# Gated feed-forward of a decoder block: activations in two float32r parts in place of three bf16 ones, three sets of gate and up banks, two banks for the down products

## The chip, the cores and the metric

The kernel runs on one core of one Trainium2 chip. The metric is the device time of one execution in microseconds; the median of three runs is 887.89 us (886.81 to 888.18). Engines: TensorE (PE in the profile, its weight loads PEld), VectorE (DVE), ScalarE (ACT), GpSimd (POOL) and SyncE (SP), which here only issues DMAs.

## The reference

Eight batches of 256 tokens with 256 features go through two decoder layers: a gated recurrence, a cross attention, a ternary feed-forward, a self attention with relative positions, a masked cross attention, and last a gated feed-forward. Only the last is touched. Per batch, with x the output of the masked attention after its layer norm:

```
gate = x @ (Wg_int / 127).T          # 256 -> 768
up   = x @ (Wu_int / 127).T          # 256 -> 768
y    = x + (silu(gate) * up) @ (Wd_int / 127).T     # 768 -> 256
out  = layernorm(y)
```

The weights are integers from -127 to 127, which bf16 holds exactly. Activations are float32. The kernel before writes each activation as a sum of three bf16 numbers (high, middle, low), multiplies all three by the weights and adds up in PSUM, so that the product is as good as a float32 one.

## The kernel before

The work is ordered by hand: each engine has its own program, and semaphores tie them. The feed-forward (in `attention_mask`, L1343 and on) works on pairs of batches: 512 tokens are one matmul's moving side. There are four pairs and six blocks of 128 hidden features (HT = 6), so 24 groups n = 6 p + m.

- **gate_up(n)**, TensorE, L1473: 6 matmuls for gate and 6 for up (two halves of the 256 features, three parts), 128x128 weights against 512 tokens, into banks 2 (n mod 2) and 2 (n mod 2) + 1. It waits until the products of group n-2 have read these banks.
- **tanh(n)**, ScalarE, L1708: tanh of the gate bank.
- **hidden(n)**, VectorE, L1820: two products, (tanh + 1) * gate (L1824) and that times up (L1830), into one of two buffers `hid_two`. The second waits for lo_made of group n-2, that is until GpSimd has read the buffer.
- **high(n)** on ScalarE (L1715, bf16 copy), **rest(n)** on VectorE (L1834, hidden minus high), **middle(n)** on ScalarE (L1721, bf16 copy of the rest), **low(n)** on GpSimd (L1962, rest minus middle, to bf16).
- **down(t)**, TensorE, L1500: for batch t, 2 token tiles x 6 blocks x 3 parts = 36 matmuls, the activation block stationary, 256 columns of the weights moving. It waits for all six low(n) of the pair. Banks 4 to 7 are used in turn.
- **out_begin(t)**, **out_end(t)**, VectorE, L1840 and L1867: residual, statistics, normalisation; **out_inverse(t)** on GpSimd between them (L1969).
- **split_x(b, i)**, GpSimd, L1945: the four steps that write the three parts of x of batch b. **cast_weights** (L1937) turns the integers into bf16 during batch 1 of the attention.

The order on ScalarE in the loop over n:

```python
                for n in range(1, NG):
                    tanh(n)
                    ...
                    middle(n - 1)
                    high(n)
```

VectorE does rest(n-1) and then hidden(n); out_begin follows hidden(n) for n mod 6 = 3 and 4, out_end for n mod 6 = 5 and 0. The first groups are mixed with the last attention batch: gate_up(0) stands in `fourth_round(7)`, gate_up(1) before weigh(31) (L1600), and up to gate_up(5) TensorE has turn_back, transposes and the output projection of batch 7 between the groups. VectorE has normalise(7, 0) and (7, 1) after hidden(2) and hidden(3), and norm_begin of batch 7 after hidden(5). GpSimd has normalise(7) after low(4). down(2p-2) stands after gate_up(6p+2) and down(2p-1) after gate_up(6p+3). At the end down for batches 6 and 7 runs over blocks 0 to 3 first, then 4 and 5 as their low parts come.

Of the kernel before, what the change touches and what calls it, by code (L numbers as in the profile page):

```python
# [17 lines left out]
BF16 = mybir.dt.bfloat16  # L18
I32 = mybir.dt.int32
# [7 lines left out]
P = 128  # L27
B, S, D = 8, 256, 256
H, DH = 16, 16
HID = 768  # L30
# [65 lines left out]
def decoder_kernel(nc, xT, ctxT, fside, mask0, mask1, wmats, cols_d, rows_d, gb, gate_up, down,  # L96
                   ident_d, rel_k_d, rel_v_d, mix_d, consts_d, out):
    ctx = ExitStack()
    with ctx:
# [9 lines left out]
        zero_cell = sb("zero_cell", [1, 1])  # L109
        x_feat = sb("x_feat", [P, FT, B * S])  # L110
        x_tok = sb("x_tok", [P, B, TT, D])
        c_feat = sb("c_feat", [P, FT, B * S])
        w_all_mats = sb("w_all_mats", [P, len(WMATS), FT, D])
        W = {n: w_all_mats[:, i, :, :] for i, n in enumerate(WMATS)}
# [120 lines left out]
        def glu_weights():  # L235

            return (dist[:, 0, 0:6, :].rearrange("p h s -> p (h s)").rearrange("p (k n) -> p k n", k=FT),
                    dist[:, 0, 6:12, :].rearrange("p h s -> p (h s)").rearrange("p (k n) -> p k n", k=FT),
                    dist[:, 1, 0:6, :])

        dist = sb("dist", [P, TT, H, S])
        ones_w = sb("ones_w", [P, P])
        bnd = sb("bnd", [P, TT, H * NBAND])
        dist_pairs = dist[:, :, :, :].rearrange("p t h s -> p t (h s)")\
            .rearrange("p t (e s v) -> p t e s v", e=H // 2, v=2)
        rw = sb("rw", [P, TT, H // FT // 2, RW, 2])
# [1096 lines left out]
        def attention_mask(sa_y_mm, sa_y_steps, sa_biased, sa_kept, sa_xt_mm, sa_xt_sb, sa_r_out):  # L1343
# [14 lines left out]
            x_steps, w_cast, g_mm, u_mm, th_sb, prod, h_made, hi_sb, r_made, mid_sb, lo_made = (  # L1358
                sem(f"glu_{n}") for n in ("x_steps", "w_cast", "gate_mm", "up_mm", "tanh", "product", "hidden",
                                          "high", "rest", "middle", "low"))  # L1360
# [3 lines left out]
            w_cells = rw[:, :, :, :, :].rearrange("p t e w v -> p (t e w v)")[:, 0:3 * FT * HID // 2].bitcast(BF16)  # L1364
# [3 lines left out]

            def cells(area, pattern):

                return area.rearrange(pattern).bitcast(BF16)

            x_parts = [cells(a, "p h s -> p (h s)").rearrange("p (k n) -> p k n", k=FT)
                       for a in (dist[:, 1, H // 2:H, :], dist[:, 0, 0:H // 2, :], dist[:, 0, H // 2:H, :])]
            PAIR = 2 * S
            h_high = cells(w_all_mats[:, 2:8, :, :], "p i k n -> p (i k n)").rearrange("p (a m t) -> p a m t", a=2, m=HT)
            h_mid = c_feat[:, :, :].rearrange("p k n -> p (k n)")[:, 0:HT * PAIR].bitcast(BF16)\
                .rearrange("p (a m t) -> p a m t", a=2, m=HT)
            h_low = [cells(dist[:, 1, 0:HT, :], "p h s -> p (h s)").rearrange("p (m t) -> p m t", m=HT),
                     bnd[:, :, :].rearrange("p t w -> p (t w)")[:, 0:HT * S].bitcast(BF16)  # L1380
                     .rearrange("p (m t) -> p m t", m=HT)]
# [8 lines left out]
            def part_of(part, n, lo, hi):  # L1390

                p, m = divmod(n, HT)
                if part == 2:
                    return h_low[p % 2][:, m, lo:hi]
                return (h_high, h_mid)[part][:, p % 2, m, lo:hi]

            def down_bank(t, tt):

                if t < B - 2:
                    return bank[4 + t % 4][:, tt * D:(tt + 1) * D]  # L1400
                return bank[((6, 7), (4, 5))[t % 2][tt]][:, 0:D]
# [32 lines left out]
            def mask_pe(pe):  # L1434
# [38 lines left out]
                def gate_up(n):  # L1473
# [17 lines left out]
                def down_steps(t, tt, ks):  # L1491

                    p, lo = t // 2, t % 2 * S + tt * P
                    for k in ks:
                        for i in range(3):
                            last = pe.matmul(down_bank(t, tt), part_of(i, HT * p + k, lo, lo + P), w_down[:, k, :],  # L1496
                                             start=(k == 0 and i == 0), stop=(k == HT - 1 and i == 2))
# [147 lines left out]
            def mask_act(act):  # L1645
# [62 lines left out]
                def tanh(n):  # L1708
# [3 lines left out]
                    act.activation(th_two[n % 2], bank[2 * (n % 2)][:, :], ACT.Tanh, scale=0.5 * UNIT)\  # L1712
# [20 lines left out]
                for n in range(1, NG):  # L1733
# [7 lines left out]
                    middle(n - 1)  # L1741
                    high(n)
                middle(NG - 1)

            def mask_dve(dve):
# [74 lines left out]
                def hidden(n):  # L1820
# [4 lines left out]
                                             in1=bank[2 * (n % 2)][:, :], op0=ALU.add, op1=ALU.mult)\  # L1825
# [5 lines left out]
                                             in1=bank[2 * (n % 2) + 1][:, :], op0=ALU.mult, op1=ALU.mult)\  # L1831
                        .then_inc(h_made, 1)

                def rest(n):  # L1834

                    dve.wait_ge(hi_sb, n + 1)
                    dve.tensor_tensor(hid_two[n % 2], hid_two[n % 2], part_of(0, n, 0, PAIR), ALU.subtract)\
                        .then_inc(r_made, 1)

                def out_begin(t):  # L1840
# [5 lines left out]
                    if t < B - 2:  # L1846
                        step(dve.scalar_tensor_tensor(
                            out=y_two[i][:, :, :], in0=bank[4 + t % 4][:, :].rearrange("p (t f) -> p t f", t=TT),
# [30 lines left out]
                for n in range(1, NG):  # L1879
                    rest(n - 1)  # L1880
# [16 lines left out]
                rest(NG - 1)  # L1897
# [6 lines left out]
            def mask_pool(pool):  # L1904
# [40 lines left out]
                def split_x(b, i):  # L1945

                    whole = batch(x_feat, b)
                    high, mid, low = (batch(part, b) for part in x_parts)
                    if i == 0:
                        pool.wait_ge(xt_sb, b + 1)  # L1950
                        pool.wait_ge(w_cast, 3)
                        pool.tensor_copy(high, whole).then_inc(x_steps, 1)
                        return
                    pool.wait_ge(x_steps, 4 * b + i)
                    if i == 1:
                        pool.tensor_tensor(whole, whole, high, ALU.subtract).then_inc(x_steps, 1)
                    if i == 2:
                        pool.tensor_copy(mid, whole).then_inc(x_steps, 1)
                    if i == 3:
                        pool.tensor_tensor(low, whole, mid, ALU.subtract).then_inc(x_steps, 1)  # L1960
# [15 lines left out]
                for b in range(B):  # L1976
# [7 lines left out]
                    if b >= 3:  # L1984
                        for i in range(4):
# [4 lines left out]
                for n in range(NG):  # L1990
# [1190 lines left out]
```

## Time and profile before

| | |
|---|---|
| median of 3 runs | 887.89 us (886.81 to 888.18) |
| span of the profiled execution | 885.5 us, clock 0.999 |
| TensorE busy | 847.8 us (96%), 7018 instructions |
| VectorE busy | 680.2 us (77%) |
| ScalarE busy | 618.7 us (70%) |
| GpSimd busy | 417.6 us (47%) |

The profiled execution's span counts from its first to its last instruction; the run's time lies 2.4 us above it. Busy shares are averages over six layers with different limits; the feed-forward is the stretch from about 774 us to the end.

### The profile page before, as it was taken

To read this page: it belongs to the slowest core of one execution; us is meant where nothing else is said; L and a number is where in the kernel's file an instruction comes from. 1 tells how busy PE (TensorE), PEld (TensorE's weight loads), DVE (VectorE), ACT (ScalarE), POOL (GpSimd) and SP (SyncE) were. 2 spreads that over 40 slices of the span, in tenths; PEclk is the share of its full clock that TensorE was granted. 3 is DMA by queue.
4 is the path that set the end of the run, shared out by engine and by line. 5 is a ranking of instruction groups with operands and counts; after the bars stand their busy time and mean duration, and the time that the engine had idled before them with its cause. 6 is when DMAs were issued, how large, how long until landed. Compare 5 with 4: busy or idle time off the path is not lost.

```text
span 885.5 us, 21124 instructions
## 1 busy us (share of the span) xinstructions
PE 847.8 (96%) x7018; PEld 613.6 (69%) x7029; DVE 680.2 (77%) x2504; ACT 618.7 (70%) x1605; POOL 417.6 (47%) x447
## 2 busy tenths in 40 slices
PE   9998999999989989999999999999999999999996
PEld 7876777777768667777676766767666766746554
DVE  4988798888997767787686766838888888866876
ACT  4547877777872578787787777748888888854441
POOL 1256546775451345435455342245445555346532
PEclk9999999999999999999999999999999999999999
DMA  9444100000005388797796877760010000000001
GB/s 323 138 119 120 46 24 26 26 25 14 14 13 215 96 279 267 228 283 229 213 283 204 269 231 231 202 210 4 28 29 28 28 29 26 2 1 1 25 24 48
DMA packets 96993, 101.89 MB, mean 115 GB/s; under 512 B 26910, under 2 KB 92190, under 8 KB 96631
## 3 DMA queue, kind: packets, MB, share of 16 engines
q1 hardware_dynamic: 96324, 100.20, 36.4%
q8 instruction: 58, 0.95, 0.4%
q14 instruction: 49, 0.39, 0.2%
q10 hardware_dynamic: 562, 0.35, 0.1%
HBM read 48.70 MB, written 51.82 MB: 114 GB/s over the span
## 4 chain that ended last, share of the span: by engine, by line
PE 46%; ACT 7%; DMA 5%; DVE 4%; issue 2%; SPq 2%; POOL 1%; DVEq 0%; ACTq 0%
PE bank L1445 6%; PE bank L223 5%; PE bank L1486 5%; PE bank L231 4%; PE bank L1429 4%; PE bank L2144 3%; PE bank L1496 3%; PE bank L1460 2%; PE bank L2130 2%; PE bank L2161 2%; ACT bias_area L2482 2%; PE bank L2194 2%; PE bank L2238 2%; PE bank L2232 1%; DMA dist<-skew_scratch 1%
## 5 line engine op out<-in xcount | busy, mean ns | idle before, releaser
L223 PE MATMUL bank<-x_feat,w_all_mats 128*128 128x256 f32 x384 | 93.2, 387 | 2.1 <-ACT q_full L341 0.6
L2879 POOL TENSOR_TENSOR bnd<-bnd,consts 128x60 f32<-128x60 f32 x64 | 18.1, 305 | 142.5 <-DMA bnd<-band_scratch 142.5
L223 PEld LDWEIGHTS bank<-x_feat,w_all_mats 128*128 128x128 f32 x384 | 70.3, 190 | 15.1 <-ACT rw L2524 3.8
L2482 ACT ACTIVATE bias_area<-bias_area,mq_two 128x256 f32<-128x256 f32 x128 | 66.4, 531 | 0.0
L1486 PE MATMUL bank<-dist,rw 128*128 128x512 bf16 x277 | 63.1, 379 | 0.6
L866 ACT ACTIVATE q_heads<-bank 128x512 f32<-128x512 f32 x64 | 37.7, 589 | 34.6 <-PE bank L682 34.6
L2658 DVE COPY q_heads<-bank 128x512 f32<-128x512 f32 x64 | 41.3, 683 | 22.4 <-PE bank L2144 22.4
L1764 DVE COPY q_heads<-bank 128x512 f32<-128x512 f32 x64 | 42.1, 685 | 19.3 <-PE bank L1445 19.2
L1651 ACT ACTIVATE Sx<-Sx,mq 128x256 f32<-128x256 f32 x128 | 54.3, 499 | 3.4 <-DVE mq L1756 3.4
L858 ACT ACTIVATE Sx<-Sx,mq 128x256 f32<-128x256 f32 x128 | 54.4, 498 | 3.0 <-DVE mq L944 3.0
L952 DVE COPY q_heads<-bank 128x512 f32<-128x512 f32 x64 | 41.9, 684 | 18.3 <-PE bank L682 18.3
L858 ACT ACTIVATE Pr<-Pr,mq 128x256 f32<-128x256 f32 x128 | 54.3, 501 | 0.9 <-DVE mq L944 0.9
L1651 ACT ACTIVATE Pr<-Pr,mq 128x256 f32<-128x256 f32 x128 | 54.4, 503 | 0.0
L1756 DVE CUSTOM_DVE_ANT_0 Sx<-bank,bias_area 128x256 f32<-128x256 f32 x128 | 46.6, 421 | 7.4 <-PE bank L1429 4.1
L2500 ACT ACTIVATE w_all_mats<-bank 108x512 f32<-108x512 f32 x32 | 19.0, 595 | 46.7 <-PE bank L2176 46.7
L1659 ACT ACTIVATE q_heads<-bank 128x512 f32<-128x512 f32 x64 | 37.7, 590 | 19.1 <-PE bank L1445 18.5
L944 DVE CUSTOM_DVE_ANT_0 Sx<-bank,bias_area 128x256 f32<-128x256 f32 x128 | 46.5, 420 | 4.7 <-PE bank L668 4.2
L1486 PEld LDWEIGHTS bank<-dist,rw 128*128 128x128 bf16 x288 | 28.2, 98 | 31.3
L231 PE MATMUL bank<-w_all_mats,aT 128*128 128x256 f32 x192 | 46.9, 387 | 1.4 <-ACT q_full L881 1.3
L2650 DVE CUSTOM_DVE_ANT_0 bias_area<-bank,dist 128x256 f32<-128x256 f32 x128 | 46.7, 421 | 1.2 <-DMA dist<-skew_scratch 1.0
L944 DVE CUSTOM_DVE_ANT_0 Pr<-bank,bias_area 128x256 f32<-128x256 f32 x128 | 46.9, 419 | 0.0
L1756 DVE CUSTOM_DVE_ANT_0 Pr<-bank,bias_area 128x256 f32<-128x256 f32 x128 | 46.5, 420 | 0.0
(288 smaller groups left out, 2451.9 us busy)
## 6 DMA issues: line engine op xcount, KB each, us to landing
dist<-skew_scratch SPq DMA_DIRECT2D x64, 296.0 KB, 4.4
skew_scratch<-rw SPq DMA_DIRECT2D x30, 588.0 KB, 4.4
bnd<-band_scratch SPq DMA_DIRECT2D x64, 108.0 KB, 2.8
band_scratch<-bias_area SPq DMA_DIRECT2D x32, 162.0 KB, 2.9
band_scratch<-bias_area SPq DMA_DIRECT2D x32, 148.0 KB, 2.6
skew_scratch<-dist SPq DMA_DIRECT2D x4, 1024.0 KB, 8.4
context_values<-dist SPq DMA_DIRECT2D x8, 512.0 KB, 2.6
v_two<-context_values SPq DMA_DIRECT2D x8, 512.0 KB, 3.5
```

The costliest lines, as they stand in the source:

```text
L223: last = pe.matmul(dst[:, m * S:(m + 1) * S], w[:, k, m * P:(m + 1) * P], rhs[:, k, :], start=(k == 0), stop=(k == FT - 1))
L231: last = pe.matmul(dst[:, t * D:(t + 1) * D], src[:, k, t * P:(t + 1) * P], w[:, k, :], start=(k == 0), stop=(k == FT - 1))
L858: last = act.activation(rows_of(g, t), rows_of(g, t), ACT.Exp, bias=mq[:, g, t:t + 1], scale=-1.0)
L944: dve.tensor_tensor_reduce(out=rows_of(g, t), in0=s_bank[g][:, t * S:(t + 1) * S], in1=bias_two[:, b % 2, t, :], scale=-1.0, scalar=3e38, ...
L952: dve.tensor_copy(PTq[:, 4 * (n % 2) + g, :, :], t_bank[g % 2][:, :].rearrange("p (k q) -> p k q", k=TT))\
L1445: last = pe.transpose(t_bank[g % 2][:, k * S + t * P:k * S + (t + 1) * P], rows_of(g, t)[:, k * P:(k + 1) * P], ident[:, :])
L1486: last = pe.matmul(dst[:, :], w_[:, k, m * P:(m + 1) * P], x_parts[i][:, k, p * PAIR:(p + 1) * PAIR], start=(k == 0 and i == 0), stop=(k = ...
L1651: last = act.activation(rows_of(g, t), rows_of(g, t), ACT.Exp, bias=mq[:, g, t:t + 1], scale=-1.0)
L1756: dve.tensor_tensor_reduce(out=rows_of(g, t), in0=s_bank[g][:, t * S:(t + 1) * S], in1=x1_bias_two[:, b % 2, t, :], scale=-1.0, scalar=3e3 ...
L1764: dve.tensor_copy(PTq[:, 4 * (n % 2) + g, :, :], t_bank[g % 2][:, :].rearrange("p (k q) -> p k q", k=TT))\
L2482: last = act.activation(rows_of(n, g)[:, t, :], rows_of(n, g)[:, t, :], ACT.Exp, bias=mq_two[:, n % 2, g, t:t + 1], scale=-1.0, accum_out= ...
L2650: dve.tensor_tensor_reduce(out=rows_of(n, g)[:, t, :], in0=s_bank[g][:, t * S:(t + 1) * S], in1=dist_pairs[:, t, 2 * j + g // 2, :, g % 2] ...
```

## The change

The parts become two numbers of type float32r, a four-byte type that an engine rounds to when it writes it: high = round(value), low = value - high. All 12 matmuls of gate_up become 8, the 36 of down(t) become 24. rest(n) and middle(n) go; low(n) is hidden minus high and follows high(n). split_x has two steps instead of four. The weights are cast in place (int32 to float32r in `dist`), and the parts lie in other areas, so some buffers are laid out in another order. gate and up have three sets of banks (0 to 5), down two banks (6 and 7; for the last batch 0 and 1). x parts have room for two pairs, so the split of pair p waits for the up products of pair p-2.

```diff
-                        pe.wait_ge(x_steps, 4 * 2 * (p + 1))
-                    for w_, dst, done, free in ((w_gate, bank[2 * (n % 2)], g_mm, prod),
-                                                (w_up, bank[2 * (n % 2) + 1], u_mm, h_made)):
-                        ge(pe, free, n - 1)
+                        pe.wait_ge(x_steps, 2 * 2 * (p + 1))
+                    for w_, dst, done, free in ((w_gate, gate_bank(n), g_mm, prod), (w_up, up_bank(n), u_mm, h_made)):
+                        ge(pe, free, n - 2)
                         for k in range(FT):
-                            for i in range(3):
+                            for i in range(2):
                                 last = pe.matmul(dst[:, :], w_[:, k, m * P:(m + 1) * P],
-                                                 x_parts[i][:, k, p * PAIR:(p + 1) * PAIR],
-                                                 start=(k == 0 and i == 0), stop=(k == FT - 1 and i == 2))
+                                                 x_two[p % 2][:, i, k, :],
+                                                 start=(k == 0 and i == 0), stop=(k == FT - 1 and i == 1))
...
                     for k in ks:
-                        for i in range(3):
+                        for i in range(2):
                             last = pe.matmul(down_bank(t, tt), part_of(i, HT * p + k, lo, lo + P), w_down[:, k, :],
...
                     pe.wait_ge(lo_made, HT * (t // 2 + 1))
-                    ge(pe, n_steps2, 4 * (t - 4) + 1)
-                    if t == 3:
+                    ge(pe, n_steps2, 4 * (t - 2) + 1)
+                    if t == 1:
                         pe.wait_ge(xt_sb, B)
...
+            def gate_bank(n):
+
+                return bank[2 * (n % 3)]
+
+            def up_bank(n):
+
+                return bank[2 * (n % 3) + 1]
...
-                def middle(n):
-
-                    act.wait_ge(r_made, n + 1)
-                    act.activation(part_of(1, n, 0, PAIR), hid_two[n % 2], ACT.Copy).then_inc(mid_sb, 1)
...
-                    middle(n - 1)
                     high(n)
-                middle(NG - 1)
...
-                def rest(n):
-
-                    dve.wait_ge(hi_sb, n + 1)
-                    dve.tensor_tensor(hid_two[n % 2], hid_two[n % 2], part_of(0, n, 0, PAIR), ALU.subtract)\
-                        .then_inc(r_made, 1)
...
                 for n in range(1, NG):
-                    rest(n - 1)
                     hidden(n)
...
+                        ge(pool, u_mm, HT * (p - 1))
+                        pool.tensor_copy(high, batch(x_feat, b)).then_inc(x_steps, 1)
+                    else:
+                        pool.wait_ge(x_steps, 2 * b + 1)
+                        pool.tensor_tensor(low, batch(x_feat, b), high, ALU.subtract).then_inc(x_steps, 1)
...
                 def low(n):
 
-                    pool.wait_ge(mid_sb, n + 1)
+                    pool.wait_ge(hi_sb, n + 1)
                     ge(pool, d_mm, 2 * (n // HT - 1))
-                    pool.tensor_tensor(part_of(2, n, 0, PAIR), hid_two[n % 2], part_of(1, n, 0, PAIR), ALU.subtract)\
+                    pool.tensor_tensor(part_of(1, n, 0, PAIR), hid_two[n % 2], part_of(0, n, 0, PAIR), ALU.subtract)\
                         .then_inc(lo_made, 1)
...
-                    if b >= 3:
-                        for i in range(4):
+                    if 3 <= b < B - 1:
+                        for i in range(2):
                             split_x(b - 3, i)
...
-                    if n in (0, 1, 2, 4):
-                        split_x(B - 3, (0, 1, 2, 4).index(n))
-                    if n in (5, 6, 7, 8):
-                        split_x(B - 2, (5, 6, 7, 8).index(n))
-                    if n in (11, 12, 13, 14):
-                        split_x(B - 1, (11, 12, 13, 14).index(n))
+                    for b, after in ((B - 4, 6), (B - 3, 8), (B - 2, 12), (B - 1, 14)):
+                        if n in (after, after + 1):
+                            split_x(b, n - after)
```

## Rows read from the trace of the kernel before

**Rows 1.** The core's span and its mean granted TensorE clock.

```profile
core 0: 885.5 us, clock 0.999
```

**Rows 2.** Busy time by stretch: PE, PEld, DVE, ACT, POOL; clock, DMA share, GB/s.

```profile
843.40:866.80 23.40, 23.24 (x143) 14.07 (x144) 17.31 (x34) 10.48 (x19) 8.30 (x8) 1.00 0.07 23
866.80:885.50 18.70, 11.55 (x90) 8.51 (x87) 12.47 (x34) 3.97 (x7) 6.30 (x7) 0.94 0.17 57
```

**Rows 3.** Timeline of TensorE: start us, length us, operation, count.

```profile
769.96 1.04 PE L1445 MATMUL bank<-ident,Pr 128*128 128x128 f32 x8
...
796.96 1.89 PE L231 MATMUL bank<-w_all_mats,aT 128*128 128x256 f32 x8
798.69 7.93 PE L1486 MATMUL bank<-dist,rw 128*128 128x512 bf16 x35
806.46 0.60 PE L215 MATMUL bank<-ident,x_tok 128*128 128x128 f32 x4
```

**Rows 4.** The chain that ended last, the last down products.

```profile
870.50 6.56 PE bank L1496 x60
```

**Rows 5.** Timeline of VectorE; in brackets idle time before, and what ended it.

```profile
781.00 0.69 DVE L1824 SCALAR_TENSOR_TENSOR q_par<-k_two,bank 128x512 f32<-128x512 f32 x1 [3.51 <-ACT k_two L1712]
...
798.99 0.69 DVE L182 TENSOR_TENSOR y_sb<-bank,x_tok 128x512 f32<-128x512 f32 x1
...
801.28 0.69 DVE L1837 TENSOR_TENSOR q_par<-q_par,w_all_mats 128x512 f32<-128x512 f32 x1
...
807.97 0.69 DVE L1830 SCALAR_TENSOR_TENSOR q_par<-q_par,bank 128x512 f32<-128x512 f32 x1 [2.70 <-POOL dist L1966]
...
821.80 0.68 DVE L1847 SCALAR_TENSOR_TENSOR at<-bank,x_tok 128x512 f32<-128x512 f32 x1
...
823.74 0.68 DVE L1837 TENSOR_TENSOR q_par<-q_par,w_all_mats 128x512 f32<-128x512 f32 x1
...
825.66 1.14 DVE L1873 TENSOR_SCALAR xn<-y_sb,mv,rstd 128x256 f32<-128x256 f32 x2
...
856.40 0.68 DVE L1824 SCALAR_TENSOR_TENSOR q_par<-k_two,bank 128x512 f32<-128x512 f32 x1
857.11 0.69 DVE L1830 SCALAR_TENSOR_TENSOR q_par<-q_par,bank 128x512 f32<-128x512 f32 x1
...
871.85 0.69 DVE L1830 SCALAR_TENSOR_TENSOR q_par<-q_par,bank 128x512 f32<-128x512 f32 x1
...
877.08 0.76 DVE L1852 SCALAR_TENSOR_TENSOR y_sb<-bank,x_tok 128x256 f32<-128x256 f32 x2 [2.24 <-PE bank L1496]
```

**Rows 6.** Timeline of ScalarE.

```profile
780.38 0.59 ACT L1712 ACTIVATE k_two<-bank 128x512 f32<-128x512 f32 x1
783.51 0.38 ACT L1668 ACTIVATE w_all_mats<-bank 128x256 f32<-128x256 f32 x1 [2.54 <-PE bank L1460]
783.79 0.62 ACT L1719 ACTIVATE w_all_mats<-q_par 128x512 bf16<-128x512 f32 x1
...
855.13 0.63 ACT L1719 ACTIVATE w_all_mats<-q_par 128x512 bf16<-128x512 f32 x1 [0.69 <-DVE q_par L1830]
855.67 0.58 ACT L1712 ACTIVATE k_two<-bank 128x512 f32<-128x512 f32 x1
...
857.84 0.63 ACT L1719 ACTIVATE w_all_mats<-q_par 128x512 bf16<-128x512 f32 x1 [0.69 <-DVE q_par L1830]
```

**Rows 7.** Groups by line and form: busy us, mean ns of a weight load.

```profile
L231 PEld LDWEIGHTS bank<-w_all_mats,aT 128*128 128x128 f32 x192 | 34.7, 190 | 12.0 <-issue 8.1
...
L1486 PEld LDWEIGHTS bank<-dist,rw 128*128 128x128 bf16 x288 | 28.2, 98 | 31.3
L1445 PEld LDWEIGHTS bank<-ident,Pr 128*128 128x128 f32 x256 | 27.8, 141 | 8.5 <-ACT Pr L1651 6.3 <-issue 2.0
```

**Rows 8.** Timeline of GpSimd.

```profile
801.45 1.09 POOL L1929 TENSOR_TENSOR rstd<-ve,neghalf 128x2 f32<-128x2 f32 x1 [2.03 <-DVE ve L197]
...
805.57 1.15 POOL L1960 TENSOR_TENSOR dist<-x_feat,dist 128x512 bf16<-128x512 f32 x1
...
874.94 1.16 POOL L1966 TENSOR_TENSOR bnd<-q_par,c_feat 128x512 bf16<-128x512 f32 x1 [1.12 <-ACT c_feat L1724]
```

More of the change, by code:

```diff
@@ L18 @@
 BF16 = mybir.dt.bfloat16
+F32R = mybir.dt.float32r
 I32 = mybir.dt.int32
@@ L1356, in attention_mask @@
                 s_(n) for n in ("norm_steps", "normed", "y_steps", "rstd", "kept"))
-            x_steps, w_cast, g_mm, u_mm, th_sb, prod, h_made, hi_sb, r_made, mid_sb, lo_made = (
+            x_steps, w_cast, g_mm, u_mm, th_sb, prod, h_made, hi_sb, lo_made = (
                 sem(f"glu_{n}") for n in ("x_steps", "w_cast", "gate_mm", "up_mm", "tanh", "product", "hidden",
-                                          "high", "rest", "middle", "low"))
+                                          "high", "low"))
             d_mm, n_steps2, rstd2, xn_ready = (sem(f"glu_{n}") for n in ("down_mm", "n_steps", "rstd", "xn"))
@@ L1367, in attention_mask @@
             w_down = w_down.rearrange("p (k n) -> p k n", k=HT)
[L1369 to L1381, printed above, removed]
+            x_two = [exact_cells("glu_x_even", [P, 2, FT, PAIR], dist_at + 4 * 3 * FT * HID),
+                     exact_cells("glu_x_odd", [P, 2, FT, PAIR], rw_at)]
+            h_high = [exact_cells("glu_high_even", [P, HT, PAIR], w_all_at + 4 * 2 * FT * D),
+                      exact_cells("glu_high_odd", [P, HT, PAIR], w_all_at + 4 * 8 * FT * D)]
+            low_even = exact_cells("glu_low_even", [P, HT, PAIR], c_feat_at)
+            low_odd = [exact_cells("glu_low_odd_first", [P, HT // 2, PAIR], dist_at + 4 * (3 * FT * HID + 2 * FT * PAIR)),
+                       exact_cells("glu_low_odd_last", [P, HT // 2, PAIR], bnd_at)]
             th_two = [k_two[:, i, :, :].rearrange("p k n -> p (k n)") for i in range(2)]
@@ L1392, in part_of @@
                 p, m = divmod(n, HT)
-                if part == 2:
-                    return h_low[p % 2][:, m, lo:hi]
-                return (h_high, h_mid)[part][:, p % 2, m, lo:hi]
+                if part == 0:
+                    return h_high[p % 2][:, m, lo:hi]
+                if p % 2 == 0:
+                    return low_even[:, m, lo:hi]
+                return low_odd[2 * m // HT][:, m % (HT // 2), lo:hi]
             def down_bank(t, tt):
                 if t < B - 2:
-                    return bank[4 + t % 4][:, tt * D:(tt + 1) * D]
-                return bank[((6, 7), (4, 5))[t % 2][tt]][:, 0:D]
+                    return bank[6 + t % 2][:, tt * D:(tt + 1) * D]
+                return bank[((6, 7), (0, 1))[t % 2][tt]][:, 0:D]
+            def gate_bank(n):
+                return bank[2 * (n % 3)]
+            def up_bank(n):
+                return bank[2 * (n % 3) + 1]
             NQ = H // 4
@@ L1494, in down_steps @@
                     for k in ks:
-                        for i in range(3):
+                        for i in range(2):
                             last = pe.matmul(down_bank(t, tt), part_of(i, HT * p + k, lo, lo + P), w_down[:, k, :],
-                                             start=(k == 0 and i == 0), stop=(k == HT - 1 and i == 2))
+                                             start=(k == 0 and i == 0), stop=(k == HT - 1 and i == 1))
                     return last
@@ L1711, in tanh @@
                     ge(act, prod, n - 1)
-                    act.activation(th_two[n % 2], bank[2 * (n % 2)][:, :], ACT.Tanh, scale=0.5 * UNIT)\
+                    act.activation(th_two[n % 2], gate_bank(n)[:, :], ACT.Tanh, scale=0.5 * UNIT)\
                         .then_inc(th_sb, 1)
@@ L1824, in hidden @@
                     dve.scalar_tensor_tensor(out=gt_two[n % 2], in0=th_two[n % 2], scalar=1.0,
-                                             in1=bank[2 * (n % 2)][:, :], op0=ALU.add, op1=ALU.mult)\
+                                             in1=gate_bank(n)[:, :], op0=ALU.add, op1=ALU.mult)\
                         .then_inc(prod, 1)
@@ L1847, in out_begin @@
                         step(dve.scalar_tensor_tensor(
-                            out=y_two[i][:, :, :], in0=bank[4 + t % 4][:, :].rearrange("p (t f) -> p t f", t=TT),
+                            out=y_two[i][:, :, :], in0=bank[6 + t % 2][:, :].rearrange("p (t f) -> p t f", t=TT),
                             scalar=UNIT, in1=x_tok[:, t, :, :], op0=ALU.mult, op1=ALU.add))
@@ L1945, in split_x @@
                 def split_x(b, i):
-                    whole = batch(x_feat, b)
-                    high, mid, low = (batch(part, b) for part in x_parts)
+                    p, lo = b // 2, b % 2 * S
+                    high, low = (x_two[p % 2][:, part, :, lo:lo + S] for part in range(2))
                     if i == 0:
```

37 lines of the change are left out of this document (18 added, 19 removed).

## The prediction, made before the change was run

> **What bounds the kernel now.** I first looked at the clock and the span: 885.5 us, TensorE at full clock throughout [rows 1]. The change touches only the gated feed-forward, so I then read the stretches of it. One stretch is a pair of batches in the steady part, 843.4 to 866.8: the reader is to see that TensorE is busy 23.24 of 23.40 us while VectorE, ScalarE and GpSimd have 17.3, 10.5 and 8.3 [rows 2]. The stretch behind it, 866.8 to 885.5, is the tail. TensorE's own timeline gives the pace of each form. A bf16 matmul of 512 columns starts 0.216 us after the one before: 36 of them from 798.69 to 806.46, where the next form's row would stand (35 records are shown in 7.93 us, one is missing) [rows 3]. One of 256 columns starts after 6.56/60 = 0.109 us [rows 4]. A pair of batches is 6 x 12 x 0.216 + 2 x 36 x 0.109 = 15.55 + 7.85 = 23.4 us, all of the stretch. So today this part is bound by TensorE's columns and by nothing else.
>
> **But how far off is the next bound?** The answer is not in the busy shares but in an order that the code fixes. ScalarE does tanh(n) and then high(n); high(n) waits for both VectorE products of hidden(n), which wait for tanh(n). tanh(n+1) stands behind high(n) in ScalarE's queue. So each group n is one serial round, however many banks there are. I read its four steps, start to start, where nothing else delayed them: high to the next tanh 855.13 to 855.67 = 0.54; tanh to the first product 780.38 to 781.00 = 0.62; first to second product 856.40 to 857.11 = 0.71; second product to high 857.11 to 857.84 = 0.73 [rows 5, 6]. That is 2.60 us a group. Before, 12 matmuls took 2.59, so the round was hidden.
>
> **The change, part by part.**
> (a) gate_up: 8 matmuls of 512 columns in place of 12. If a float32r matmul moves one column a cycle as bf16 does, a group takes 1.73 us and 24 groups save 24 x 4 x 0.216 = 20.7 us of TensorE time.
> (b) down: 24 of 256 columns per batch in place of 36, 2.62 in place of 3.93 us; 8 x 12 x 0.109 = 10.5 us saved. Together 31.2 us.
> The price of a float32r matmul is the big unknown, since no row has one. The nearest rows are float32: one product of 4 matmuls of 256 columns shows 8 records in 1.89 us, (1.89 - 0.387 for the last one's own length)/7 = 0.215 us each, and two records per matmul [rows 3]. A record thus moves a column in two cycles and a float32 matmul costs four. Ends for float32r: 0.216 us per 512 columns (one cycle) and 0.43 (one record at the float32 pace); above that, at four cycles, the split of the activations would buy nothing. By its bytes the new form is nearest to these rows, by its work to the bf16 ones: float32 takes four cycles for two full operands, that is two halves of each against two of the other; a part that holds about half of an activation's bits, against an integer below 128, is one of the four. I take one cycle. The Trainium skill ("FP8 and Floating Point Precision", TensorE Precision Notes) says the same: true float32 is four passes, reduced precision reads the four bytes and truncates to FP22. By that rule the sum stays at the lower end; four passes agree with the trace's 2 x 0.215 us, the reduced form no row here shows.
> Against the change speaks the weight load of the down products, where a new stationary block comes with every 256 columns. Loads last 0.098 us for bf16, 0.141 in float32 transposes and 0.190 in float32 matmuls [rows 7]; the length is not the pace: 8 float32 transposes, each with its load, take 1.04 us, (1.04 - 0.28)/7 = 0.109 us each [rows 3]. So a four-byte load repeats at least every 0.109 us, and I take 0.109 for a down matmul; the upper end is 0.215. The Trainium skill ("TensorE: Matmul & The Clock Gate", Weight-path perf modes and LDWEIGHTS) says that the fast weight load is off for float32 and that a load is columns/1.2 ns, 107 ns for 128; by that the down matmul would still come at about 0.107, so the rule would not change the sum.
> (c) The third part goes: VectorE's rest(n) (24 instructions of 0.68 us [rows 5]), ScalarE's middle(n) (24 x 0.54) and two of four split_x steps on GpSimd. None of the three engines bounds the stretch [rows 2]; it leaves the round at 2.60 (with rest in it, 855.13 to 857.84 is 2.71 [rows 6]). GpSimd's low(n), 1.16 us, now follows high(n).
> (d) Three sets of banks let TensorE be two groups ahead of the products instead of one. That hides down() behind the round; it doesn't shorten the round. Two banks for down: down(t) needs out_begin(t-2), which is long done in the walk below. down(1) now waits for turn_x(7), since it writes the bank that this reads.
> (e) split_x(4) moves from the last attention batch to groups 6 and 7; split_x(6), (7) to 12 to 15. The weights' cast stays, in place. No DMA moves.
>
> **The walk.** TensorE needs 6 x 1.73 + 2 x 2.62 = 15.6 us a pair. The round needs 6 x 2.60, plus what out_begin adds: VectorE has 2.60 - 1.31 = 1.29 us free in a round, out_begin takes 821.80 to 823.74 = 1.94 [rows 5], so each of two adds 0.66 us. out_end, 1.06 to 1.14 [rows 5], fits. A pair is 15.6 + 1.3 = 16.9 us: the bound has gone from TensorE to the serial round.
> Start: high(0) is at 783.79, right behind the copy that waits for weigh(31) [rows 6]; gate_up(0) and (1) lie before that on TensorE and save 2 x 0.86, so high(0) comes at 782.07. Five rounds: high(5) 795.07, its second product 794.35. Turning back and the two normalise fit in the rounds' gaps. normalise(7, 1) follows group 3's second product (789.15) and I give it until 790.5; transposes 0.66 (three steps of 0.109 and the last one's length), gate_up(5) 1.7, projection 1.9 [rows 3] end by 794.8. Then norm_begin, 2.29 us from 798.99 before, delays the first product of group 6 to 797.25 (a cost of 1.0), and its variance comes 4.0 us earlier than before. GpSimd's normalise(7) holds the queue from 801.45 to 805.57, 4.12 us [rows 8]; now from 797.4 to 801.5. low(5) is queued behind it and ends at 802.7, and the second product of group 7 waits for it, as one waits 2.70 us in the trace before [rows 5]: 802.75, 2.2 late. Group 9: 807.95. down(0) runs 802.8 to 805.4 (it waits for low(5)), gate_up(9) to 807.15, down(1) from 807.8 (turn_x(7)) to 810.4, so gate_up(10) comes 1.6 us late: group 10 at 812.8, group 11, with out_begin(1) in front, at 816.0. Two pairs at 16.9: group 23's second product at 849.9, against 871.85 before [rows 5].
> Tail: high(23) starts 0.73 later and lasts some 0.63 [rows 6], low(23) 1.16 [rows 8]; with the handovers 2.58, 852.45. Before it started 3.1 us after the second product, now 1.4 [rows 5, 8]. TensorE has by then done the 32 down matmuls of parts 0 to 3 (out_begin(5) lets them start near 847.7; 3.5 us). Four more and the last one's result: about 853.3 for the first VectorE read, which is at 877.08 before [rows 5]. From there on nothing changes, 8.4 us. Span 861.7, 23.8 us less. The median of the runs before is 887.9, 2.4 above the span, so 864 us.
>
> **Rivals.**
> 1. The forecast: round bound, 864. Its own bounds: 0.37 us more at each out_begin if its inner waits fall badly, 2 us; as much for contention. 860 to 870. Chance 0.68.
> 2. TensorE stays the bound with nothing lost in waits: 887.9 - 31.2 = 857. For it speaks only the sum of (a) and (b); against it the code's order on ScalarE. It would need a round under 2.6 us. 0.05.
> 3. The down matmuls are bound by their weight loads. They decide from 15.6 + 1.3 = 6 x 1.73 + 48d, d = 0.136 us. At 0.141 to 0.190 (the loads' lengths) a pair is 17.2 to 19.5 us; with the first pair and the tail's 32 about 3 to 11 us more, 867 to 875; at 0.215 it is 8 x 24 x 0.106 = 20.4 less some 5 of slack, 879. 0.13.
> 4. The other side: float32r moves a column in two cycles, as every float32 record does. gate_up is then 24 x (8 x 0.43 - 12 x 0.216) = 20.4 us longer and down 8 x (24 x 0.215 - 36 x 0.109) = 9.9 longer, 918 us; it turns slower from 1.5 cycles a column, where 8 matmuls cost as much as 12. For it: all four-byte rows here; against: the parts argued in (a). 0.14.
>
> **How the numbers follow.** 864 is the likeliest case. Cases 1, 2 and 3 up to 879 hold 0.86; from 858 to 878 about 0.8 is held. Runs before lie from 886.81 to 888.18, so 0.2% is about what can be told from no change. Faster 0.85 (cases 1 to 3), slower 0.14, same 0.01.
>
> **What would show it.** A 512-column float32r matmul at 0.216 us start to start, one record each, and a 256-column one near 0.11. A pair of batches in 16.9 us with TensorE busy about 15.6. tanh waiting for nothing from TensorE but right behind high; rounds of 2.6 us, 3.3 with out_begin. A wait of the second product of group 7 for GpSimd's low(5). The prediction is wrong if records come in pairs or at 0.43 us, or if the round is not 2.6.

## The result and the profile after

The changed kernel takes 865.93 us (median of 4 runs, 863.66 to 869.36) against 887.35 in the same comparison; the ratio is 0.9763, with a 95% interval of 0.9736 to 0.979. It is 21.4 us faster. The prediction was 864.

First the core's span and clock, then busy time by stretch (PE, PEld, DVE, ACT, POOL, clock, DMA share, GB/s), both of the changed kernel. They answer to [rows 1, 2]:

```profile
core 0: 863.6 us, clock 0.995
```

```profile
817.20:834.40 17.20, 17.20 (x100) 15.02 (x99) 13.18 (x29) 6.82 (x12) 12.80 (x13) 1.00 0.09 30
...
851.50:863.60 12.10, 4.16 (x33) 3.75 (x32) 8.09 (x23) 0.63 (x1) 3.00 (x4) 0.90 0.25 87
```

One pair of batches now takes about as long as this stretch, 17.2 us, in place of 23.4, and TensorE is shown as busy all the time in it as before. Busy time alone would say that TensorE still sets the pace. The weight loads have grown to 15.0 of 17.2 us. But the stretch holds 100 matmul records where a pair has 96 matmuls: TensorE gets through a pair's work in less than 17.2 us and runs ahead of the other engines. It had fallen behind them at group 10 and is making that good.

TensorE's timeline of the changed kernel (start, length, count), which answers to [rows 3, 4]:

```profile
823.31 2.00 PE L1501 MATMUL bank<-glu_x_even,glu_weight_cells 128*128 128x512 f32 x8
825.15 0.28 PE L1511 MATMUL bank<-glu_weight_cells,glu_high_odd 128*128 128x256 f32 x1
...
827.88 0.28 PE L1511 MATMUL bank<-glu_weight_cells,glu_low_odd_last 128*128 128x256 f32 x1
828.00 2.23 PE L1501 MATMUL bank<-glu_x_even,glu_weight_cells 128*128 128x512 f32 x9
```

Eight matmuls of 512 columns from 823.31 to 825.15 are 0.230 us each, one record per matmul; the 24 of down(3) from 825.15 to 828.00 are 0.119 each (before: 0.216 and 0.109). A pair is 6 x 8 x 0.230 + 48 x 0.119 = 11.04 + 5.71 = 16.75 us of TensorE.

The weight loads, from the changed kernel's instructions by source line (min/median/max ns), answer to [rows 7]:

```profile
L1501 PEld LDWEIGHTS bank<-glu_x_even,glu_weight_cells x96: 187/188/192, 775.8 to 831.2; 128*128 128x128 f32 x96
```

```profile
L1511 PEld LDWEIGHTS bank<-glu_weight_cells,glu_high_even x48: 186/192/193, 803.1 to 844.5; 128*128 128x128 f32 x48
```

A float32r load lasts as long as one of a float32 matmul (0.190), twice a bf16 one (0.098).

ScalarE's timeline of the changed kernel, answering to [rows 6]:

```profile
812.50 0.60 ACT L1727 ACTIVATE k_two<-bank 128x512 f32<-128x512 f32 x1 [2.60 <-PE bank L1501]
...
837.67 0.63 ACT L1734 ACTIVATE glu_high_odd<-q_par 128x512 fp32r<-128x512 f32 x1 [1.47 <-DVE q_par L1838]
838.21 0.58 ACT L1727 ACTIVATE k_two<-bank 128x512 f32<-128x512 f32 x1
840.27 0.63 ACT L1734 ACTIVATE glu_high_odd<-q_par 128x512 fp32r<-128x512 f32 x1 [1.48 <-DVE q_par L1838]
840.80 0.58 ACT L1727 ACTIVATE k_two<-bank 128x512 f32<-128x512 f32 x1
842.86 0.63 ACT L1734 ACTIVATE glu_high_odd<-q_par 128x512 fp32r<-128x512 f32 x1 [1.48 <-DVE q_par L1838]
```

Here is the serial round: high at 837.67, 840.27, 842.86, so 2.60 us apart; tanh starts 0.54 behind high with no wait of its own, and high waits 1.48 us for the second product. Tanh waits for TensorE only twice: 2.60 us in group 10, behind down(0) and down(1), and 0.17 us at 829.12, in a round in which out_begin delays VectorE by more.

VectorE, answering to [rows 5]:

```profile
803.18 0.69 DVE L1838 SCALAR_TENSOR_TENSOR q_par<-q_par,bank 128x512 f32<-128x512 f32 x1 [1.50 <-POOL glu_low_even L1962]
...
834.36 0.69 DVE L1838 SCALAR_TENSOR_TENSOR q_par<-q_par,bank 128x512 f32<-128x512 f32 x1
...
845.34 0.68 DVE L1849 SCALAR_TENSOR_TENSOR y_sb<-bank,x_tok 128x512 f32<-128x512 f32 x1
...
847.20 0.28 DVE L1866 TENSOR_SCALAR ve<-mv 128x2 f32<-128x2 f32 x1
847.39 0.67 DVE L1832 SCALAR_TENSOR_TENSOR q_par<-k_two,bank 128x512 f32<-128x512 f32 x1
...
851.49 0.69 DVE L1838 SCALAR_TENSOR_TENSOR q_par<-q_par,bank 128x512 f32<-128x512 f32 x1
...
855.13 0.76 DVE L1854 SCALAR_TENSOR_TENSOR y_sb<-bank,x_tok 128x256 f32<-128x256 f32 x2 [0.68 <-PE bank L1511]
```

The second product of group 7 waits for GpSimd's low(5), as forecast. Groups 17 and 23 (834.36 and 851.49) are 17.13 us apart. out_begin now takes 2.05 us (845.34 to 847.39) instead of 1.94. GpSimd, answering to [rows 8]:

```profile
798.56 0.71 POOL L1929 TENSOR_TENSOR rstd<-ve,neghalf 128x2 f32<-128x2 f32 x1 [2.64 <-DVE ve L206]
799.38 2.43 POOL L1933 TENSOR_SCALAR x_tok<-y_sb,mv,rstd 128x256 f32<-128x256 f32 x2
801.78 1.27 POOL L1962 TENSOR_TENSOR glu_low_even<-q_par,glu_high_even 128x512 fp32r<-128x512 f32 x1
...
852.92 1.38 POOL L1962 TENSOR_TENSOR glu_low_odd_last<-q_par,glu_high_odd 128x512 fp32r<-128x512 f32 x1 [1.28 <-ACT glu_high_odd L1734]
```

Two lengths are used to compare all kernels below, since the layers ahead of this stage end at moments that differ by some 3 us from one profile to the next (the first gate_up starts at 773.8 to 777.0 in all traces here, 774.85 before, 775.84 after). **Stage** is from the start of gate_up(0) to VectorE's first read of the last down products: 877.08 - 774.85 = 102.2 us before, 855.13 - 775.84 = 79.3 after. **Pair** is from the second product of group 17 to that of group 23: 23.40 before, 17.13 after. The stage is 22.9 us shorter; the median fell by 21.4.

### The profile page after: what moved, and what is told of

Same layout as the page of the kernel before. It is cut to its first block, busy times and chain, and to the rows that moved or that the text cites. A ratio compares the mean times of both kernels' runs of the same rounds, so it can differ in the third digit from the quotient of the medians.

```text
span 863.6 us, 20689 instructions
## 1 busy us (share of the span) xinstructions
PE 824.5 (95%) x6837; PEld 617.1 (71%) x6837; DVE 661.1 (77%) x2480; ACT 603.6 (70%) x1581; POOL 405.3 (47%) x431
## 4 chain that ended last, share of the span: by engine, by line
PE 47%; ACT 9%; DVE 5%; issue 2%; DMA 2%; POOL 1%; SPq 1%; DVEq 0%; ACTq 0%
PE bank L1461 6%; PE bank L232 6%; PE bank L240 5%; PE bank L2137 4%; PE bank L1445 4%; PE bank L1501 3%; ACT bias_area L2475 3%; PE bank L2123 3%; PE bank L1476 3%; PE bank L2154 2%; PE bank L2187 2%; PE bank L2231 2%; PE bank L1511 2%; PE bank L2225 2%; DMA dist<-skew_scratch 1%
## 5 line engine op out<-in xcount | busy, mean ns | idle before, releaser
L2651 DVE COPY q_heads<-bank 128x512 f32<-128x512 f32 x64 | 41.2, 683 | 22.8 <-PE bank L2137 22.8
L1461 PE MATMUL bank<-ident,Sx 128*128 128x128 f32 x256 | 38.9, 282 | 5.6 <-ACT q_heads L1674 5.1
L1461 PEld LDWEIGHTS bank<-ident,Sx 128*128 128x128 f32 x256 | 27.2, 141 | 22.7 <-issue 10.8
```

Source lines behind the costliest of these rows:

```text
L1461: last = pe.transpose(t_bank[g % 2][:, k * S + t * P:k * S + (t + 1) * P], rows_of(g, t)[:, k * P:(k + 1) * P], ident[:, :])
L2651: dve.tensor_copy(PTq[:, 4 * (n % 2) + g, :, :], t_bank[g % 2][:, :].rearrange("p (k q) -> p k q", k=TT))\
```

## Experiments

Theory R says that the pace after the change is that of the serial round on ScalarE and VectorE, with TensorE just under it. Theory T says that TensorE, shown busy in the whole pair, is still the bound. The chain that ended last, in the changed kernel, runs through TensorE's matmuls from 811.5 to 842.1 and so speaks for T:

```profile
811.53 9.09 PE bank L1501 x40
820.62 2.85 PE bank L1511 x24
823.47 1.84 PE bank L1501 x8
825.31 2.85 PE bank L1511 x24
828.16 9.21 PE bank L1501 x40
```

TensorE takes 16.63 us for this pair's matmuls (811.53 to 828.16), while the second products of groups 11 and 17 are 17.14 us apart. The two theories are 0.4 to 0.5 us a pair apart, which is little to go by in reading alone; the experiments move one limit at a time.

All runs, with stage and pair from one profile each. The kernel before, run again beside each set of these kernels, had medians of 887.4 to 888.8, so medians of different rows compare to about 1 us, and the ratio is the fairer number:

| kernel | median us | ratio to before (95%) | stage us | pair us |
|---|---|---|---|---|
| changed | 865.9 | 0.9763 (0.9736 to 0.979) | 79.3 | 17.13 |
| tanh ahead | 865.8 | 0.9749 (0.9726 to 0.9773) | 79.8 | 18.50 |
| longer round | 873.8 | 0.9839 (0.9816 to 0.9861) | 87.7 | 19.03 |
| half of down | 863.6 | 0.9732 (0.9706 to 0.9758) | 77.3 | 17.11 |
| two sets of banks | 867.2 | 0.9764 (0.9741 to 0.9787) | 80.4 | 18.01 |
| tanh ahead, all orders | 863.8 | 0.9723 (0.9701 to 0.9745) | 77.3 | 16.69 |
| half of down, tanh ahead | 856.7 | 0.9639 (0.9617 to 0.966) | 71.0 | 15.65 |
| two bf16 parts | 865.2 | 0.9738 (0.9714 to 0.9762) | 77.4 | 16.89 |
| two bf16 parts, tanh ahead | 860.9 | 0.9695 (0.9673 to 0.9718) | 75.0 | 16.91 |
| two bf16 parts, all orders | 860.6 | 0.9686 (0.9664 to 0.9707) | 73.1 | 15.60 |
| before with three sets | 887.9 | 0.9996 (0.9982 to 1.001) | 102.6 | 23.40 |

**A longer round.** A second tanh of the same bank, into an unused buffer:

```diff
+                    act.activation(Sx[:, n % 2, :, :].rearrange("p t k -> p (t k)"), gate_bank(n)[:, :], ACT.Tanh,
+                                   scale=0.5 * UNIT)
                     act.activation(th_two[n % 2], gate_bank(n)[:, :], ACT.Tanh, scale=0.5 * UNIT)\
```

> The changed kernel with a second tanh of the same gate bank into an unused buffer ahead of each tanh: ScalarE has 0.5 us more in every round and about 7.5 us busy of 17 more room than it needs. Theory R: every round that the products do not already delay becomes 0.5 us longer, 4 of 6 in a pair (in the two with out_begin VectorE is the later one by 0.8): 2 us a pair, 19.1 in place of 17.1; with the first twelve groups 6 to 9 us in all, 872 to 875. Theory T: ScalarE is half idle, so 0 to 2 us.

Measured: 873.8 us, the stage 8.4 us and the pair 1.90 us longer. ScalarE's timeline of this kernel:

```profile
841.81 0.63 ACT L1736 ACTIVATE glu_high_odd<-q_par 128x512 fp32r<-128x512 f32 x1 [1.48 <-DVE q_par L1840]
842.35 0.58 ACT L1727 ACTIVATE Sx<-bank 128x512 f32<-128x512 f32 x1
842.83 0.59 ACT L1729 ACTIVATE k_two<-bank 128x512 f32<-128x512 f32 x1
...
844.89 0.63 ACT L1736 ACTIVATE glu_high_odd<-q_par 128x512 fp32r<-128x512 f32 x1 [1.48 <-DVE q_par L1840]
```

The added 0.48 us (842.35 to 842.83) appears whole in the round, 3.08 in place of 2.60, four times a pair (1.92). ScalarE is idle for about half of this pair (9.6 us busy of 19.0; in the changed kernel 6.8 of 17.2), and still the added time counts in full in these rounds. That is what R says.

**Half of down.** The low parts are left out of the down products:

```diff
-                        for i in range(2):
+                        for i in range(1):
                             last = pe.matmul(down_bank(t, tt), part_of(i, HT * p + k, lo, lo + P), w_down[:, k, :],
-                                             start=(k == 0 and i == 0), stop=(k == HT - 1 and i == 1))
+                                             start=(k == 0 and i == 0), stop=(k == HT - 1 and i == 0))
```

> The changed kernel with the low parts left out of the down products (12 matmuls a batch in place of 24; low is still computed). TensorE has 2.9 us less a pair. Theory R: a pair stays at 17.1 us; only where TensorE was late (group 10, behind down(0) and down(1)) and in the tail something is gained, 2 to 4 us in all, 862 to 864. Theory T: 2.9 us in each of four pairs, 11 us, 855.

Measured: 863.6 us, a pair 17.11 us. Two rows of this kernel, TensorE's timeline in one pair, and the busy times of nearly the same stretch:

```profile
827.98 4.39 PE L1501 MATMUL bank<-glu_x_odd,glu_weight_cells 128*128 128x512 f32 x12 [2.60 <-POOL glu_x_odd L1956]
```

```profile
813.60:830.70 17.10, 14.50 (x70) 12.02 (x69) 13.08 (x29) 6.71 (x12) 12.72 (x13) 0.91 0.09 31
```

TensorE has 24 matmuls less, stands for 2.60 us until the split of x is done, and even gets a mean clock of 0.91 in the stretch, and the pair that runs from 813.62 to 830.70 is 17.08 us long, as before the edit. T's 11 us aren't there. The 2.0 us by which the stage is shorter are in the groups up to 10 (1.6) and in the tail (0.3), as expected.

**Both lifted.** The same with tanh(n) ahead of high(n-1):

> The changed kernel with tanh(n) before high(n-1), and the low parts left out of the down products (12 matmuls a batch). Both limits are lifted at once. Theory R: TensorE has 13.9 us a pair and VectorE some 13; a pair falls from 17.1 to about 14 to 15, in all 5 to 8 us less than the changed kernel, 858 to 861, whereas either edit alone gave 0 and 2 us. If the order on ScalarE were no limit, this would give no more than leaving out the low parts alone: 863.6.

Measured: 856.7 us, 9.2 less than the changed kernel and more than the 5 to 8 expected, though the two pairs, 15.18 and 15.65, are longer than the 14 to 15 expected. By the stage it is 8.3 us: 4.6 up to group 11, 3.4 in the two pairs and 0.3 in the tail. In the stage one edit gave nothing (tanh ahead alone, shown next, was 0.5 longer), the other 2.0 us, both together 8.3: two limits that lie close to each other hide each other.

**tanh ahead alone.**

```diff
                 copy_ot(NQ * B - 1)
-                high(0)
                 for n in range(1, NG):
                     tanh(n)
...
-                    high(n)
+                    high(n - 1)
+                high(NG - 1)
```

> The changed kernel with one edit: ScalarE does tanh(n) before high(n-1), so high is no longer between two tanh. Theory R (the serial round tanh, two products, high of 2.60 us sets the pace, 17.1 us a pair; TensorE needs 6 x 1.84 + 48 x 0.119 = 16.8 us): the round goes, TensorE takes over, a pair falls to about 16.8 us, and the first twelve groups, where TensorE waits for the products, gain 1 to 3 us; in all 2 to 4 us less than the changed kernel, 862 to 864. Theory T (TensorE's float32r columns and loads set the pace already): no change, 866.

Measured: 865.8 us; the 2 to 4 us that I expected under R did not come. Who waited for whom in this kernel (total us, times, longest), and one row of TensorE's timeline:

```profile
ACT k_two L1727 <- PE bank L1501: 34.7, 20, 3.7
```

```profile
830.94 1.43 PE L1501 MATMUL bank<-glu_x_odd,glu_weight_cells 128*128 128x512 f32 x5 [1.08 <-POOL glu_x_odd L1956]
```

In the changed kernel the same wait has 2.8 us in two times. So the round is open, tanh now waits for TensorE 20 times, and TensorE itself waits 1.1 us for the split of x at two of the pairs' starts, and behind GpSimd's normalise(7) as before. The expectation took R's other limit to be TensorE alone; there was a third. ScalarE and GpSimd ahead of that row:

```profile
827.17 0.60 ACT L1727 ACTIVATE k_two<-bank 128x512 f32<-128x512 f32 x1 [3.57 <-PE bank L1501]
827.66 0.62 ACT L1734 ACTIVATE glu_high_even<-q_par 128x512 fp32r<-128x512 f32 x1
```

```profile
828.36 1.29 POOL L1962 TENSOR_TENSOR glu_low_even<-q_par,glu_high_even 128x512 fp32r<-128x512 f32 x1 [2.83 <-ACT glu_high_even L1734]
829.62 1.26 POOL L1956 TENSOR_TENSOR glu_x_odd<-x_feat,glu_x_odd 128x512 fp32r<-128x512 f32 x1
```

The edit brings this limit on itself: high(15) now stands behind tanh(16), which waits 3.57 us for TensorE, GpSimd's low(15) waits for high(15), and the last step of the split of x stands behind low(15). In the changed kernel that step ended at 831.59, just before TensorE's first matmul of the pair at 831.65. The first groups did gain what was expected (group 11's second product comes 39.6 us after the stage's start instead of 41.4), and the two pairs lost 2.2 us (18.02 and 18.50).

**All three orders.** The same, with normalise(7) after low(5) and the splits one group earlier:

```diff
-                    if n == 4:
+                    if n == 5:
                         normalise(B - 1)
-                    for b, after in ((B - 4, 6), (B - 3, 8), (B - 2, 12), (B - 1, 14)):
+                    for b, after in ((B - 4, 5), (B - 3, 7), (B - 2, 11), (B - 1, 13)):
```

> The changed kernel with three edits of order: tanh(n) before high(n-1) on ScalarE; GpSimd's normalise(7) after low(5) instead of ahead of it; the splits of x one group earlier (groups 5 to 8, 11 to 14). Since the edit of ScalarE alone left the time where it was, with two waits of TensorE of 1.1 us each for x parts, theory R says that three limits lie close together (round 17.1, TensorE 16.75, x parts) and that with all three moved TensorE sets the pace: pairs of about 16.8 us and 77.5 us from the first gate_up to the last stage's first VectorE read, in place of 79.3; 864. Rival: the loss is contention or something that order does not mend: 866 and pairs of 17 to 18 us.

Measured: 863.8 us, the stage 77.3 (77.5 expected), a pair 16.69. The chain that ended last, in this kernel:

```profile
822.13 2.85 PE bank L1511 x24
824.97 9.10 PE bank L1501 x40
834.07 2.87 PE bank L1511 x24
836.94 1.84 PE bank L1501 x8
838.78 2.87 PE bank L1511 x24
```

TensorE runs without a gap, at 16.65 us a pair (822.13 to 838.78), near the 16.75 worked out above. So here, and not in the changed kernel, TensorE sets the pace. The median lies 2.1 us under the changed kernel's; the intervals of the two ratios overlap (0.9701 to 0.9745 and 0.9736 to 0.979), the stage lengths say it more clearly. Which of the two added edits is needed was not tried. It is the fastest version here that keeps float32r's bits.

**Two sets of banks.** The banks of before with the rest of the change (two sets for gate and up, four for down, and their waits):

```diff
-                return bank[2 * (n % 3)]
+                return bank[2 * (n % 2)]
...
-                        ge(pe, free, n - 2)
+                        ge(pe, free, n - 1)
...
-                    ge(pe, n_steps2, 4 * (t - 2) + 1)
+                    ge(pe, n_steps2, 4 * (t - 4) + 1)
```

> The changed kernel with the banks of before: two sets of gate and up banks, four banks for down. Theory R: TensorE may be one group ahead instead of two; down(2p-1) then makes the next tanh about 0.6 us late in a pair, less where out_begin delays it anyway, and more in the first pair: 1 to 3 us slower than the changed kernel, 867 to 869. Rival: the third set carries the gain, since down() is in the way of the round without it: 2 x 1.5 us a pair, 6 us or more, 872 and up. Second rival: it is worth nothing, 866.

Measured: 867.2 us, the stage 1.1 and a pair 0.88 us longer. Between 810 and 848 us TensorE waits for a bank to be read, which it does not once in the changed kernel (total us, times, longest):

```profile
PE bank L1501 <- DVE q_par L1832: 1.4, 4, 0.5
```

By stage and median this is at the lower end of the 1 to 3 expected. The ratio is that of the changed kernel (0.9764 and 0.9763), so that the third set is worth about 1 us rests on one profile of each, and the second rival, nothing, is not ruled out. That it carries the gain is ruled out.

**The banks alone.** The kernel before, three bf16 parts, with three sets and two down banks (the same edits the other way):

> The kernel before with the change's banks alone: three sets of gate and up banks, two banks for down; three bf16 parts, rest and middle as they were. Theory: with three parts TensorE needs 23.4 us of the 23.4 of a pair, so a further set of banks has nothing to hide; 0 to 1 us less (some small waits in the first groups), 887 to 888. Rival: the banks alone give part of the change's gain: 3 us or more.

Measured: 0.9996 (0.9982 to 1.001), a pair 23.40. Nothing: TensorE had no gap that a bank could fill. With the run before, in which the parts alone gave a ratio of 0.9764, this says that the gain comes from the parts, not from the banks.

**The price of a float32r matmul.** The changed kernel with the type bf16 for weights and both parts (fewer bits of an activation are kept), weights in `rw` and the odd pairs' x in `dist`:

```diff
-                return nc.alloc_sbuf_tensor_at(name, shape, F32R, offset=at)
+                return nc.alloc_sbuf_tensor_at(name, shape, BF16, offset=at)
```

> The changed kernel with its weights and both parts in bf16 instead of float32r (two bf16 parts carry fewer bits of an activation; the weights lie in rw again, x of the odd pairs in dist). It isolates the price of a float32r matmul: 0.216 against 0.230 and 0.109 against 0.119 us, 16.75 to 15.6 us a pair on TensorE. Theory R: pairs stay at 17.1 us, since the round sets them; 0 to 2 us less in the first pair and the tail, 864 to 866. Theory T (float32r's price sets the pace): 4 x 1.15 = 4.6 us less, 861.

TensorE's timeline of this kernel:

```profile
839.37 1.89 PE L1501 MATMUL bank<-glu_x_odd,glu_weight_cells 128*128 128x512 bf16 x8
```

(1.89 - 0.379)/7 = 0.216 us a matmul, against (2.00 - 0.39)/7 = 0.230 with float32r in the same place. So float32r costs 6% more at 512 columns and 9% more at 256, 1.15 us a pair on TensorE. Measured: 865.2 us, not the 861 of T. The stage is 1.9 us shorter, 1.0 of it up to group 10; the pair got only 0.24 us shorter, and that is out_begin's step (below), not the matmuls: in a pair the dearer matmul is hidden behind the round.

With tanh ahead as well:

> The same as the run before it, two bf16 parts, with tanh(n) before high(n-1) on ScalarE. The round is open, TensorE needs 15.6 us a pair. Theory R: 16 to 16.8 us a pair with the waits for x parts, 3 to 5 us less than the changed kernel, 861 to 863. If the order is no limit: as with two bf16 parts alone.

Measured: 860.9 us, the stage 4.3 us shorter than the changed kernel's. The pair, 16.91, is a little over the 16 to 16.8 expected, with TensorE waiting 0.97 us for the split of x at two pairs' starts. And with all three orders:

> Two bf16 parts (fewer bits of an activation) with the three edits of order: tanh(n) before high(n-1), normalise(7) after low(5), splits of x one group earlier. TensorE needs 15.6 us a pair in place of 16.75 with float32r. If TensorE's pace sets the time once the orders are out of the way, a pair comes to 15.7 to 16 us and the time lies 3 to 4.5 us under the same edits with float32r (863.8): 859 to 861. If something else (VectorE, the waits for x parts) is left, it stays at 16.6 or more and within 1 us of two bf16 parts with tanh ahead alone (860.9).

Measured: 860.6 us, the stage 73.1, a pair 15.60: TensorE's own 15.6. The median gained only 0.3 us over the run before it, the stage 2.0; pair and stage say what the expectation said, the median is within what such runs differ. Against the same orders with float32r (863.8) it is 3.3 us, by the stage 4.2: once the round is open, the price of float32r shows.

## Why the prediction was right

**The form's pace.** Forecast 0.216 us per 512 columns and one record each: it is 0.230, one record each. So float32r moves about one column a cycle (512 cycles at the full 2.4 GHz are 0.213 us), and the rival of two cycles (918 us) is out. The Trainium skill ("FP8 and Floating Point Precision", TensorE Precision Notes) says that true float32 is four passes and that the reduced form truncates to FP22; that the reduced form is a single pass is the prediction's inference. This trace agrees with it: 0.230 for 512 columns against 4 x 0.215 for the same in float32.

**The down matmul.** Forecast 0.109: it is 0.119. The forecast put the price from which the down matmuls would decide at 0.136; with 0.230 in gate_up it is (17.13 - 11.04)/48 = 0.127, so they don't, by a small margin. The Trainium skill ("TensorE: Matmul & The Clock Gate", LDWEIGHTS) gives 107 ns a load, which would fit under the 0.109. The trace has loads of 0.188 to 0.192 that start every 0.119 us, and doesn't show what the 10 ns are; here the measurement decides. The Trainium skill ("TensorE: Matmul & The Clock Gate", Weight-path perf modes) has the fast load off for float32, which agrees with 0.190 against 0.098; float32r's loads are as long as float32's. Whether the load is what makes it 0.119 and 0.230 wasn't tried.

**The round.** Forecast 2.60 us: measured 2.60 (837.67 to 840.27). The longer round and the half of down show that it sets the pace. Rival 2 (857, TensorE the bound) was out for the reason given, but its figure was also too low: at the real 16.75 us a pair TensorE is only 0.4 under the round, where the forecast had it 1.3 under. One sign that the prediction named, TensorE busy about 15.6 us in a pair, failed: it is busy throughout. That the time hardly shows it is partly luck, since the dearer matmul is hidden only as long as it stays under the round. The closeness was not foreseen; it leaves 0.4 us a pair to be won by opening the round, and the split of x takes that away.

**A pair.** Forecast 16.9, measured 17.13. The term is out_begin's delay: 3.37 - 2.60 = 0.77 us each instead of 0.66. The small last step of out_begin (L1866) takes 0.28 to 0.31 us in the groups, 0.17 in the tail, and in the run with two bf16 parts 0.17. That is the 0.11 us. It ends just behind GpSimd's low: in the changed kernel

```profile
850.56 0.31 DVE L1866 TENSOR_SCALAR ffn_ve<-ffn_mv 128x2 f32<-128x2 f32 x1
```

```profile
849.53 1.32 POOL L1962 TENSOR_TENSOR glu_low_odd_last<-q_par,glu_high_odd 128x512 fp32r<-128x512 f32 x1 [1.28 <-ACT glu_high_odd L1734]
```

ends at 850.87 and 850.85. So it is in all six groups of the changed kernel that have this step, 0.02 to 0.03 us behind the end of low. Where low ends earlier (847.05 in the run with two bf16 parts, with the step at 846.93) the step takes its 0.17. With tanh ahead one low lies later, and the step, at 849.04, takes 0.62 us and ends at 849.66, low at 849.63. These rows fit a step that is held until GpSimd's subtraction is over; no run tried it by itself, and what holds it they don't show.

**The first groups.** Counted from gate_up(0), whose start was taken as 774.85: group 7's second product was forecast 27.9 us later and came 27.3 later; normalise(7) took 3.2 us (798.56 to 801.78) instead of the 4.1 of the trace before. Group 10 was forecast at 37.9 and came at 38.0, group 11 at 41.2 and 41.4, group 23 at 75.1 and 75.7. That group 10 is right to 0.1 is luck: down(0) started 0.7 us earlier than forecast, for the shorter normalise(7), and the dearer matmuls had used this up by the end of down(1) (35.5 us, as forecast).

**Tail.** low(23) lasts 1.38 us instead of 1.16 and the down matmuls are dearer: 3.64 us from the last product to VectorE's read, where 3.4 was forecast. From there to the end 8.5 us, as forecast 8.4. The prediction reads the clock as full throughout; in the tail it is not (0.94 before [rows 2], 0.90 after), but after the change it is still 1.00 from 852.0 to 855.2 and falls only where TensorE has its last matmuls to do.

**The sum.** Stage forecast 853.3 - 774.85 = 78.5 us, measured 79.3. The rest of the 2 us between 861.7 and the span of 863.6 is that the layers ahead ended 1.0 us later in this profile, which lies inside the 3 us by which that moment differs between profiles.

## What to carry to other kernels

When matmuls are taken away from a full TensorE, work out the next limit as a round: write down which instruction of one group stands behind which in each engine's queue, add the four or five starts, and set the sum beside TensorE's new time. Here 31 us of matmuls were to come off by bf16's price, and the stage got 22.9 us shorter. Of the difference of 8.3 us float32r's price is some 4 (77.3 against 73.1 us with all orders), the three orders are 2.0 (79.3 against 77.3), and the first groups and the tail are the rest. ScalarE, busy 40% of the time, had tanh(n+1) behind high(n), and with this order a pair got no shorter when TensorE's work was cut further. When the two sums lie close together, expect that mending one alone shows nothing, and judge the edits by a stretch of the trace rather than by the median.

## What the hardware showed that was not expected

- A float32r matmul of 512 columns takes 0.230 us and one of 256 columns 0.119, against 0.216 and 0.109 in bf16, with weight loads of 0.19 against 0.098 us.
- A GpSimd subtraction of 128x512 takes 1.27 to 1.32 us with float32r output, 1.38 once, against 1.16 with bf16 output. ScalarE's copy is 0.63 us with either.
- A VectorE step of 128x2 elements, 0.17 us by itself, that started during a GpSimd subtraction of 128x512 lasted up to 0.62 us and ended within 0.05 us of its end (rows under "A pair").
- With half of down left out, TensorE's mean granted clock is 0.91 in a stretch in which it stood still for 2.60 us, from 825.4 to 828.0. The clock has two levels, 1.2 and 2.4 GHz, and the loss lies right behind the stand, in this row of that kernel (clock 0.51, 7 matmuls in 3 us where 13 would fit at 0.230); from 831 on it is 1.00 again. The pair took the same time, since TensorE was not the limit there. Behind a stand of 1.08 us, with tanh ahead, the clock stayed at 1.00.

```profile
828.00:831.00 3.00, 3.00 (x7) 2.43 (x8) 2.79 (x9) 1.12 (x2) 2.55 (x3) 0.51 0.00 0
```
